# Filling the next table of sums in a graph network: the bias rows read from a full tile instead of from one repeated row

## What is computed

```python
def _gcn_conv(x, src, dst, ew, W, b):          # L0, three times
    ...
    msg = norm[:, None] * h[src2]
    out = jax.ops.segment_sum(msg, dst2, num_segments=N)
    return out + b

def eve_conv(...):                             # L1, twice
    ...
    return x @ wself.T + eve @ weve.T + bias

def sage_conv(x, src, dst, W_l, W_r, b, n):    # L2, twice
    agg = segment_mean(x[src], dst, n)
    return agg @ W_l.T + b + x @ W_r.T
```

## Time and profile before

| what | us |
|---|---|
| median of 3 runs | 16443.93 (16431.26 to 16447.2) |
| the profiled execution | 16521.8 |
| its span, first to last instruction | 16520.0 |
| convolution stages m0, m1, m2 | about 1310 to 6300 |
| n3 | about 6340 to 6960 |
| m4, m5, m6, m7 | about 6960 to 13780 |
| g8 | about 13780 to 16520 |
| POOL busy | 7996.3 (48%) |
| DVE busy | 7053.9 (43%) |
| PE busy | 6115.5 (37%) |

### The profile page before, as it was taken

How to read it: one execution, slowest core, us unless ns; L and a number is a source line. 1 busy time by engine, 2 the same in 40 slices (tenths; PEclk the granted TensorE clock), 3 DMA queues, 4 the chain that set the end, 5 groups by cost and what they waited for, 6 DMA issues and landing times. The chain is left out here.

```text
span 16520.0 us, 161843 instructions
## 1 busy us (share of the span) xinstructions
PE 6115.5 (37%) x34188; PEld 5051.6 (31%) x34189; DVE 7053.9 (43%) x16428; ACT 4501.9 (27%) x8261; POOL 7996.3 (48%) x8118
## 2 busy tenths in 40 slices
PE   1003445454544551044444444333333333233332
PEld 0003444344434441033333333233333332122221
DVE  3203334333333337833334545232333333666666
ACT  0001111111111114422223333222223332454444
POOL 5675444444444443445544444445444445454453
PEclk5556777677777775567766767666666666666666
DMA  7204555566656666644445554454545553222222
GB/s 170 28 0 132 170 165 173 169 203 201 195 175 198 201 203 230 207 154 155 152 145 167 170 173 163 138 165 157 161 157 177 175 172 102 90 94 85 88 86 72
DMA packets 1863399, 2485.40 MB, mean 150 GB/s; under 512 B 276169, under 2 KB 1389409, under 8 KB 1863178
## 3 DMA queue, kind: packets, MB, share of 16 engines
q1 hardware_dynamic: 1134182, 1595.70, 30.5%
q10 hardware_dynamic: 490660, 512.06, 9.2%
q0 software_dynamic: 238336, 375.36, 8.0%
HBM read 1467.11 MB, written 1077.53 MB: 154 GB/s over the span
## 5 line engine op out<-in xcount | busy, mean ns | idle before, releaser
L1176 POOL DMA_INDIRECT sums_gcn<-m_result,m_idx x1176 | 1242.2, 1056 | 2198.8 <-DVE m_result L1445 1838.4
L1701 DVE SCALAR_TENSOR_TENSOR m_acc<-m_n_out,m_scales,m_res_b 128x128 f32<-128x128 f32 (+1 forms) x2352 | 643.1, 343 | 2644.9 <-remote 1688.6
L1310 ACT ACTIVATE m_nodeT<-m_n_turn 128x512 f32<-128x512 f32 x980 | 570.6, 595 | 4118.8 <-PE m_n_turn L1283 2482.4
L1176 POOL DMA_INDIRECT sums_eve<-m_result,m_idx x784 | 834.7, 1065 | 1550.9 <-DVE m_result L1530 1325.7
L1176 POOL DMA_INDIRECT sums_sage<-m_result,m_idx x784 | 774.7, 988 | 1512.6 <-DVE m_result L1445 1285.9
L1283 PE MATMUL m_n_turn<-k_ident,m_in_y 128*128 128x128 f32 x5488 | 1004.3, 331 | 1126.6 <-issue 497.0
L1168 POOL DMA_INDIRECT m_rows<-node_rows_a,m_idx x1176 | 1152.5, 980 | 339.6 <-issue 338.9
L1283 PEld LDWEIGHTS m_n_turn<-k_ident,m_in_y 128*128 128x128 f32 x5488 | 779.4, 172 | 1379.7 <-issue 626.8
L1295 PE MATMUL m_n_out<-k_sage_r,m_nodeT 128*128 128x128 f32 x3136 | 590.4, 362 | 1643.0 <-DVE m_z L1805 1085.1
L1646 PE MATMUL m_gram<-m_y 128*128 128x129 f32 (+1 forms) x4800 | 744.5, 302 | 876.1 <-issue 772.6
L1295 PEld LDWEIGHTS m_n_out<-k_sage_r,m_nodeT 128*128 128x128 f32 x3136 | 547.8, 269 | 1671.3 <-issue 1671.3
(11 more groups left out here) (279 smaller groups left out, 17146.6 us busy)
## 6 DMA issues: line engine op xcount, KB each, us to landing
m_in_sums<-sums_gcn SPq DMA_DIRECT2D x291, 512.0 KB
m_in_y<-node_rows_a SPq DMA_DIRECT2D x291, 512.0 KB
sums_gcn<-k_gcn_b SPq DMA_DIRECT2D x194, 512.0 KB
node_rows_a<-m_y ACTq DMA_DIRECT2D x194, 512.0 KB
m_in_x<-in_x_dram SPq DMA_DIRECT2D x194, 512.0 KB
m_in_y<-node_rows_b SPq DMA_DIRECT2D x194, 512.0 KB
sums_eve<-k_eve_b SPq DMA_DIRECT2D x194, 512.0 KB
m_in_sums<-sums_eve SPq DMA_DIRECT2D x194, 512.0 KB
```

Source lines behind the costliest of these rows:

```text
L1176: pool.indirect_dma_start(self.node_sums[:, :], bass.IndirectOffsetOnAxis(self.idx[s][:, T + t:T + t + 1], 0), self.result[b][:, t, :], No ...
L1310: act.activation(out, src, ACT.Copy).then_inc(self.n_turn_read, 1)
L1701: ins = dve.scalar_tensor_tensor(out=self.acc[b][0:n, tt, :], in0=ph.node_out(i, n)[:, t, :], scalar=self.scales[b][0:n, tt:tt + 1], in1=s ...
```

## The change

A convolution with a fill gets one more tile in SBUF, `fill_rows`, of 128 partitions by 8 by 128 elements. DVE writes it once at the start of the stage by a copy of the bias row spread over the 8 slots, and SP waits for that copy before its first transfer of the stage. The fills then read 4096 bytes in a row from each partition instead of 512 bytes eight times. Nothing is reordered: DVE has one copy more in each of the seven stages, SP has one wait more, and the fills are issued at the same places.

```diff
+        if self.fill_table is not None:
+            self.fill_rows, self.fill_made = self.sb("fill_rows", [P, T, D]), self.sem("fill_made")
         return self
 
+    def make_fill(self, dve):
+        if self.fill_table is not None:
+            dve.tensor_copy(self.fill_rows[:, :, :], spread_slots(self.fill_row[:, :], [P, T, D])).then_inc(self.fill_made, 1)
+
+    def have_fill(self, sp):
+        if self.fill_table is not None:
+            sp.wait_ge(self.fill_made, 1)
...
                 n = self.sh.rows(c)
-                sp.dma_start(node_rows(self.fill_table, c, self.sh),
-                             spread_slots(self.fill_row[0:n, :], [n, T, D])).then_inc(self.filled, 16)
+                sp.dma_start(node_rows(self.fill_table, c, self.sh), self.fill_rows[0:n, :, :]).then_inc(self.filled, 16)
...
         @block.sync
         def _(sp):
+            ph.have_fill(sp)
             merged_sweep(sp, k, sh, lambda *u: edges.sync(sp, *u), lambda *u: ph.load_nodes(sp, *u))
...
         @block.vector
         def _(dve):
+            ph.make_fill(dve)
             nodes.vector_start(dve)
```

## The result

The changed kernel took 16531.29 us, the kernel before 16459.4 in the same comparison (medians of 12 runs each): a ratio of 1.0038, with an interval of 1.0021 to 1.0055. That is 72 us more, where 4 less were forecast, and outside the range. The two profiled executions are closer together than the medians: 16533.72 us after and 16521.8 before.

A forecast was written before the change was run, and what follows sets the result against it. The prediction took each turn to be bound by POOL's DMAs and the DVE, PE and ACT chain between bursts. Its terms, -4 + 0 + 0 + 0 = -4 us, gave 16518 us profiled, 16440 median, range 16375 to 16480.

The forecast's parts named there:

- Time in the queue: SP's queue: each of 686 fills gets 0.5 us shorter (0.19 to 0.81), 343 us less queue time.
- The full stretch at the end of the turn: Sign of being right, DMA engines: their full stretch there gets 1 to 2 us shorter.
- Waits for the sums: Waits for the sums to land, 155 us in 49: a gain of 4 us, from 0 to 49.
- SP's issue: SP issuing fills: 275 ns less for each of 686, 189 us of SP, counted as 0 on the time.
- the copy: Start of seven stages: a DVE copy of 1.2 us each, hidden, so 0; 10 us if uncovered.
- the end of a stage: SP's wait there for its fills: hidden, 0; bound from 0 to a gain of 7 times 0.8 us.
- They can matter only through the queue, by what lands late behind them: SP's queue: fills are in neither POOL's burst nor the DVE, PE and ACT chain, and matter only by transfers behind them.
- the step on which the forecast was said to rest: POOL in each turn: its 173 waits stay at about 25.7 us and its burst at about 41.4 us.
- three signs that were named for being wrong: POOL's waits shorter by 1 us or more, its early burst DMAs longer, or packets still 1.13 million.
- The second rival: POOL's burst: large fill packets delay its first three DMAs by 0.21 us each, 109 us slower, 16553; chance 8%.
- The first rival: SP's queue is on the path in each of 173 turns: gain 173 us, 16271, or 66 us, 16378; chance 14%.

The follow-up runs named there:

- full_in_rest: Changed kernel with the full tile read in m4 to m7 alone, the one bias row read in m0 to m2 as before: 0.9995 of before.
- two_tiles: Changed kernel, but in m0 to m2 ACT copies each result into a second tile without ones and stores 4096 bytes in a row: 1.0003 of before.
- copy_only: Changed kernel with the full tile made and waited for, but fills reading the one bias row, 512 bytes at a time: 0.9991 of before.
- small_loads: Changed kernel with SP's loaded tiles in m0 to m2 one column wider, so loads move 512 bytes while fills keep 4096: 1.0029 of before.
- early_gcn: Kernel before with the three tables of m0 to m2 filled in the degree stage instead, leaving no fills in m0 to m2: 1.0075 of before.
- paused_full: Changed kernel with 12 spare POOL writes ahead of each edge chunk's gathers in m0 to m2: 14321 us, against 14332 for the kernel before so paused.

## Why the prediction was wrong

- *Time in the queue*: right. 0.38 us for a fill, within 0.19 to 0.81, in its lower half; 521682 packets, 1.6 points of share. The full stretch at the end of the turn is some 2 us shorter. Four microseconds at the same place of the turn, 14 us later, have a share of 0.53 where the earlier trace rows have 0.99:

```profile
2114.00:2118.00 4.00, 2.85 (x18) 2.20 (x17) 3.61 (x10) 0.00 (x0) 1.28 (x2) 0.79 0.53 195
```

- *Waits for the sums*: the forecast gain of 4 us is not seen; the waits of `m_in_sums` that the list names are 57.0 us in GCN, 77.3 in eve and 34.0 in sage, where the earlier trace rows have 57.8, 65.6 and 31.9, and the waits without a named releaser are 871.0 instead of 802.7. The kernels with the full tile and no starved stores, full_in_rest and two_tiles, are at 0.9995 and 1.0003.
- *SP's issue, the copy, the end of a stage*: right, at no cost that can be seen: copy_only is at 0.9991. The copy takes 0.69 us where 1.2 were taken, and the first user of `m_w_all` in m0 starts no later.
- *What failed*: the step "They can matter only through the queue, by what lands late behind them". It looked at what stands behind the fills in SP's queue. What suffered stood beside them, in ACT's queue. The stores were not a term of the sum at all, which put them at nothing without a reason, though the page had them: q10 with 490660 packets for 512 MB. In their place ACT waited 76.4 us for them instead of 27.3, and m2 ended 49.3 us later; on the fast kind it waited 936 us instead of 91, and 270 us were lost. With it fell the step on which the forecast was said to rest: POOL's waits went from 4450 us in 173 to 4489.4 in 171. None of the three signs that were named for being wrong came up; waits that get longer were not among them.
- *The second rival*, large packets in POOL's way, had a rule of the right kind, that a large packet of one queue holds up a small one of another. It was priced for one victim, the scatters at the start of a burst, at 0.21 us each. Their first one takes 1.15 us before and after, so that place costs nothing; that its 109 us came near the 72 measured is luck. The rule has to be run over every queue that is active at the time. Here the one that paid was ACT's, with 512-byte packets and two tiles. An engine drains a whole packet before it turns to another queue, as the Trainium skill has it ("DMA: Bandwidth & Descriptors", section "Queues, rings and completion order"). The runs agree in direction (91, 661, 929 and 936 us of waits with larger packets). The page's packet is a group of descriptors, 9 to 17 as a rule, and no run shows whether it is what the profile counts as a packet.
- *The first rival* (queue on the path, faster) fell: POOL's waits did not shorten.
- *What is left open*: that late stores cost time is shown by runs on the fast kind. On the slow kind, where the 72 us were measured, it rests on the two profiles: no run there takes the waits away and gets the time back (small_loads has 2.4 us of waits and 1.0029). The profiles give 49.3 us by the end of m2. They cannot give the rest. After is 67.0 us behind at the first `m_z` of m4 and 70.3 at the last of m7, and why the first turns of m4 add to it stays open; then g8, where nothing was changed, takes 58 us less, and its waits of POOL fall from 1080.0 to 1007.6 us. So the two spans differ by 11.9 us only, and single executions differ by as much as is sought.

```profile
POOL sums_gat L1992 <- DVE g_result L2252: 1080.0, 24, 92.6
```

```profile
POOL sums_gat L2001 <- DVE g_result L2261: 1007.6, 25, 75.9
```

## What to carry to other kernels

Before making the transfers of one queue larger in their packets, list the packet size of every queue that runs at the same time: the transfer that gets cheaper can take engine time from those with small packets, and a store with two tiles of buffer turns that into a stall of the engine that writes them. Make the packets of the waiting queue large first (here that took 936 us of waits to 13), and then the others. Whether the stall costs time depends on the slack of a turn: 936 us of waits cost 270 where POOL hardly pauses, and 280 us cost nothing where it is held up by 26 us in each turn. A transfer that looks like pure overhead may be the gap in which another queue catches up: test by taking it away, as early_gcn did.

## What the runs showed of the hardware that was not expected

The same kernel before took 12508 to 12526 us on three chips and 16234 to 16459 in two other comparisons, with the same work and the same DMA instructions; the mean granted clock was 0.71 to 0.77 in the first and 0.66 to 0.71 in the second. One chip was used twice, an hour and a half apart, and had 12525 and 12526 us; whether it is the chip or a state of it was not tested otherwise. The difference is visible in PE while POOL issues its DMAs. On the slow kind, in the second turn of m0, from the profile of before:

```profile
1513.82 0.38 PE L1646 MATMUL m_gram<-m_y 128*128 128x129 f32 x1 [2.47 <-issue]
1516.65 0.38 PE L1646 MATMUL m_gram<-m_y 128*128 128x129 f32 x1 [2.45 <-issue]
1518.75 0.37 PE L1646 MATMUL m_gram<-m_y 128*128 128x129 f32 x1 [1.73 <-issue]
```

and on the fast kind, from copy_only, also during a burst of POOL:

```profile
1737.17 3.84 PE L1653 MATMUL m_gram<-m_y 128*128 128x129 f32 x32
```

On the one, 1.7 to 2.5 us in which nothing that the profile names is waited for stand ahead of each of these products of 0.38 us; on the other 32 of them take 3.84 us. POOL's pauses of 25 us in the earlier trace rows belong to the slow kind: in GCN copy_only has 60.6 us of POOL's waits for DVE, not 1838.4. The prediction read them as the chain of DVE, PE and ACT, and did not ask why that chain was slow. That the gaps of PE make the pauses is argued from the order of the chain; their cause was not found, and no run tests it. It matters for the result: the pauses are slack in each turn, and by paused_full such slack hides late stores. That fits a cost of 0.38% there and 2.1% on the fast kind.
